# Nine phases of a transformer chain in one block: at each phase border a wait on one semaphore in place of a barrier of all engines

## The reference

```python
x = L0(x, ctx)          # one softmax over projected context rows, a gate, then a normalization
x = L1(x, ctx, mask)    # causal self-attention, cross-attention, gated feed-forward;
                        #   each token uses the "v" or the "l" weights, by the mask
x = L2(x, ctx, mask2)   # cross-attention with 16 heads of 64, then a feed-forward with gelu
x = L3(x, ctx, mask)    # as L1, with weights of its own
```

## Time and profile before

| what | value |
|---|---|
| median of 3 runs (lowest to highest) | 2504.32 us (2503.06 to 2508.76) |
| the profiled execution, its own time | 2509.57 us |
| its span, first to last instruction | 2507.8 us |
| granted TensorE clock, mean over the span (1 is 2.4 GHz, 0.5 is 1.2 GHz) | 0.96 |
| busy: PE, DVE, ACT, POOL | 2311.2, 1410.7, 1143.7, 653.1 us |
| moved by DMA | 85.55 MB |

### The profile page before, as it was taken

How to read it: one execution, slowest core, us unless ns; L and a number is a source line. 1 busy time by engine, 2 the same in 40 slices (tenths; PEclk the granted TensorE clock), 3 DMA queues, 4 the chain that set the end, 5 groups by cost and what they waited for, 6 DMA issues and landing times. The chain is left out here.

```text
span 2507.8 us, 63604 instructions
## 1 busy us (share of the span) xinstructions
PE 2311.2 (92%) x24286; PEld 1890.0 (75%) x24287; DVE 1410.7 (56%) x2866; ACT 1143.7 (46%) x2585; POOL 653.1 (26%) x833
## 2 busy tenths in 40 slices
PE   5994999997996999799999997998999998997998
PEld 4673788875765999688888876996888875666998
DVE  3563666664775333466666655554666665764433
ACT  2553444443664333334344344445444435664332
POOL 1333222212662222111111110001222214652222
PEclk9996999997998999899999998998999998998999
DMA  5440000002003111300000001000000002001111
GB/s 179 58 58 9 18 15 15 15 15 71 27 27 93 55 58 57 110 2 2 2 2 2 2 2 35 0 0 14 15 15 15 15 13 79 27 30 51 59 59 42
DMA packets 78468, 85.55 MB, mean 34 GB/s; under 512 B 19891, under 2 KB 69376, under 8 KB 78112
## 3 DMA queue, kind: packets, MB, share of 16 engines
q1 hardware_dynamic: 56016, 41.55, 7.3%
q10 hardware_dynamic: 13856, 19.61, 2.4%
q0 software_dynamic: 8368, 21.15, 2.4%
HBM read 52.22 MB, written 21.40 MB: 29 GB/s over the span
## 5 line engine op out<-in xcount | busy, mean ns | idle before, releaser
L1184 POOL TENSOR_TENSOR s_kx<-s_qkt,const 128x512 f32<-128x512 f32 x128 | 131.7, 1049 | 447.3 <-ACT s_qkt L1115 447.3
L2150 PE MATMUL ps_all<-f_wh,f_xh 128*128 x396 | 155.2, 392 | 10.6 <-DVE f_xl L2295 10.6
L1536 POOL TENSOR_TENSOR c_kx<-c_qkt,const 128x512 f32<-128x512 f32 x128 | 130.5, 1037 | 118.2 <-ACT c_qkt L1480 118.0
L534 POOL TENSOR_TENSOR a_probs<-a_probs,a_sm 128x1024 f32<-128x1024 f32 x32 | 60.9, 1902 | 384.6 <-DVE a_sm L529 384.6
L1123 ACT ACTIVATE s_pt<-ps_all 128x512 f32<-128x512 f32 x128 | 69.7, 594 | 186.9 <-PE ps_all L1005 186.9
L2151 PE MATMUL ps_all<-f_wh,f_xl 128*128 x396 | 149.3, 377 | 0.0
L2152 PE MATMUL ps_all<-f_wl,f_xh 128*128 x396 | 149.2, 377 | 0.0
L1874 ACT ACTIVATE self_w<-ps_all,a_q_bias 128x256 f32<-128x256 f32 x128 | 53.7, 470 | 196.5 <-PE ps_all L1722 196.5
L2290 DVE SCALAR_TENSOR_TENSOR f_h<-ps_all,rstd,f_act_g 128x688 f32<-128x688 f32 x66 | 61.6, 934 | 143.9 <-PE ps_all L2152 131.9
L2175 PE MATMUL ps_all<-f_dh,f_hh 128*128 x396 | 116.9, 295 | 4.0 <-DVE f_hl L2305 4.0
L505 DVE TENSOR_REDUCE s_mx<-ps_all 128x8 f32<-128x512 f32 x128 | 82.5, 686 | 61.3 <-PE ps_all L991 61.3
(11 more groups left out here) (322 smaller groups left out, 7518.7 us busy)
## 6 DMA issues: line engine op xcount, KB each, us to landing
s_v_swap<-s_v_own SPq DMA_DIRECT2D x128, 68.0 KB, 2.0
f_x_in<-x_sorted SPq DMA_DIRECT2D x66, 128.0 KB, 2.0
x_res<-x_sorted SPq DMA_DIRECT2D x66, 128.0 KB, 2.1
x_sorted<-x_res POOLq DMA_DIRECT2D x1, 4224.0 KB, 16.5
l_rows<-in_x SPq DMA_DIRECT2D x32, 128.0 KB, 3.6
x_res<-in_x SPq DMA_DIRECT2D x32, 128.0 KB, 7.4
x_res<-x_back SPq DMA_DIRECT2D x1, 3584.0 KB, 20.5
l_rows<-in_ctx SPq DMA_DIRECT2D x32, 64.0 KB, 4.3
```

The source lines that it names most:

```text
L1184: ins = nc.gpsimd.tensor_tensor(kx[:, p % 2, c], qkt[:, p % 2, 2 + c].rearrange("p (b k) -> p b k", b=2).unsqueeze(2) .broadcast_to([P, 2, ...
L1536: ins = nc.gpsimd.tensor_tensor(kx[:, p % 2, b], qkt[:, p % 2, 1, b * S:b * S + S].unsqueeze(1).broadcast_to([P, RH, S]), const[:, C_H8X:C ...
L2150: nc.tensor.matmul(bank, x_high, wh[:, w_at], start=(c == 0), stop=False)
```

## The change

All nine phases now stand in one block. Each engine's function of each phase begins with `previous_done(eng)`: a wait until `res_ok` has reached the value that the phases so far add up to, which is the last residual of the phase before (layer 0 has none before it and does not wait). The barriers at the eight inner borders are gone; the one behind the preparation and the one at the end stay. The rest of each phase is the same text, four columns further left. Cut to the pattern, with one phase of six functions:

```diff
@@ -256,6 +256,11 @@
+        def previous_done(eng):
+
+            if res_ok.base > 0:
+                eng.wait_ge(res_ok.handle, res_ok.at(0))
+
...
@@ in layer0, and alike in the five other phase functions @@
-                with nc.Block() as block:
-                    @block.sync
-                    def _(sp):
-                        def step(p, u):
+                @block.sync
+                def _(sp):
+                    previous_done(sp)
+                    def step(p, u):
...
-                    @block.gpsimd
-                    def _(pool):
+                @block.gpsimd
+                def _(pool):
+                    previous_done(pool)
...
-        for k, (phase, _) in enumerate(phases):
-            def load_next(eng):
-                if k + 1 < len(phases):
-                    phases[k + 1][1](eng, weights_in[(k + 1) % 2].handle)
-            phase(weights_in[k % 2], load_next)
+        with nc.Block() as block:
+            for k, (phase, _) in enumerate(phases):
+                def load_next(eng):
+                    if k + 1 < len(phases):
+                        phases[k + 1][1](eng, weights_in[(k + 1) % 2].handle)
+                phase(weights_in[k % 2], load_next)
```

More of the change, by code:

```diff
@@ new lines, in _, with spread, rstd_, put_sorted @@
+                @block.gpsimd
+                def _(pool):
+                    previous_done(pool)
+                    nc.gpsimd.memset(eps_f[:], CHD * 1e-6).then_inc(hpad_ok.handle, 1)
+                    def spread(p):
+                        pool.wait_ge(qkt_ok.handle, qkt_ok.at(p + 1))
+                        if s_pe.due(p - 1):
+                            pool.wait_ge(s_pe.handle, s_pe.at(p - 1))
+                        for b in range(2):
+                            ins = nc.gpsimd.tensor_tensor(
+                                kx[:, p % 2, b],
+                                qkt[:, p % 2, 1, b * S:b * S + S].unsqueeze(1).broadcast_to([P, RH, S]),
+                                const[:, C_H8X:C_H8X + RH].unsqueeze(2).broadcast_to([P, RH, S]), ALU.mult)
+                        ins.then_inc(kx_ok.handle, 1)
+                    def rstd_(g):
+                        pool.wait_ge(stat_ok.handle, stat_ok.at(g * G + G))
+                        if g == 0:
+                            pool.wait_ge(hpad_ok.handle, hpad_ok.at(1))
+                        cols = slice(g * G, g * G + G)
+                        nc.gpsimd.tensor_tensor(power[:, cols], power[:, cols], eps_f[:], ALU.add) \
+                            .then_inc(eps_ok.handle, 1)
+                        pool.wait_ge(eps_ok.handle, eps_ok.at(g + 1))
+                        nc.gpsimd.tensor_tensor(factor[:, cols], power[:, cols], half_neg[:], ALU.pow) \
+                            .then_inc(rstd_ok.handle, 1)
+                    def put_sorted(p):
+                        pool.wait_ge(res_ok.handle, res_ok.at(p + 1))
+                        pool.indirect_dma_start(x_sorted, bass.IndirectOffsetOnAxis(slot_i[:, p:p + 1], 0),
+                                                x_tile(p), None).then_inc(sorted_put.handle, 16)
+                    spread(0)
+                    spread(1)
+                    rstd_(0)
+                    for p in range(PAIRS + 3):
+                        if has(p + 2):
+                            spread(p + 2)
+                        if has(p) and p % G == G - 1 and has(p + 1):
+                            rstd_(p // G + 1)
+                        if has(p - 3):
+                            put_sorted(p - 3)
@@ new lines, in _ @@
+                @block.sync
+                def _(sp):
+                    previous_done(sp)
+                    sp.wait_ge(back_put.handle, back_put.at(0))
+                    back = x_back.rearrange("(n p) d -> p n d", p=P)
+                    for k, (lo, hi) in enumerate(((0, 4), (4, PAIRS))):
+                        sp.dma_start(x_res[:, lo * D:hi * D].rearrange("p (n d) -> p n d", d=D), back[:, lo:hi]) \
+                            .then_inc(back_in[k].handle, 16)
+                @block.tensor
@@ L1793, in dense @@
-                        def dense(p):
-                            pe.wait_ge(o_ok.handle, o_ok.at(p + 1))
-                            for c in range(J):
-                                high, low = oh[:, c * D:c * D + D], ol[:, c * D:c * D + D]
-                                nc.tensor.matmul(ps_d[:, 0:D], oth[:, c], high, start=(c == 0), stop=False)
-                                nc.tensor.matmul(ps_d[:, 0:D], oth[:, c], low, start=False, stop=False)
-                                ins = nc.tensor.matmul(ps_d[:, 0:D], otl[:, c], high, start=False, stop=(c == J - 1))
-                            ins.then_inc(d_pe.handle, 1)
@@ new lines, in _ @@
+                            proj_q(g + 1, 2 * i + 1)
+                            proj_k(g + 1, 2 * i)
+                        if has(p - 1):
+                            pv(p - 1)
+                        if more:
+                            proj_k(g + 1, 2 * i + 1)
+                        if has(p + 1):
+                            proj_v(p + 1)
+                        if i == 1 and has_group2(g + 2):
+                            xt_(g + 2)
+                        if has(p - 1):
+                            if p == 1:
+                                pe.wait_ge(wlow_ok.handle,
+                                           wlow_ok.at(len(q_splits) + len(k_splits) + len(o_splits)))
+                            dense(p - 1)
@@ new lines, in _, with rstd_ @@
+                @block.gpsimd
+                def _(pool):
+                    previous_done(pool)
+                    def rstd_(g):
+                        pool.wait_ge(stat_ok.handle, stat_ok.at(2 * g + 2))
+                        nc.gpsimd.tensor_tensor(var[:], mv[:, :, 1], eps5[:, 0:2], ALU.add).then_inc(eps_ok.handle, 1)
+                        pool.wait_ge(eps_ok.handle, eps_ok.at(g + 1))
+                        if xn_ok.due(2 * g):
+                            pool.wait_ge(xn_ok.handle, xn_ok.at(2 * g))
+                        nc.gpsimd.tensor_tensor(inv_std[:], var[:], half_neg[:, 0:2], ALU.pow).then_inc(rstd_ok.handle, 1)
+                    rstd_(0)
+                    rstd_(1)
+                    for p in range(PAIRS):
+                        softmax_norm(pool, sm, probs, p, p % 2)
+                        if p % 2 == 0 and has_group2(p // 2 + 2):
+                            rstd_(p // 2 + 2)
@@ new lines, in _ @@
+                @block.sync
+                def _(sp):
+                    previous_done(sp)
+                    sp.wait_ge(sorted_put.handle, sorted_put.at(PAIRS))
+                    for t in range(NT):
+                        if t >= 2:
+                            sp.wait_ge(xt_pe.handle, xt_pe.at(t - 1))
+                            sp.wait_ge(tile_in[t % 2].handle, tile_in[t % 2].at(t // 2))
+                        sp.dma_start(x_in[:, t % 2], x_sorted[t * P:t * P + P, :]).then_inc(tile_in[t % 2].handle, 16)
+                        sp.dma_start(rows(t), x_sorted[t * P:t * P + P, :]).then_inc(tile_in[t % 2].handle, 16)
+                    if store:
+                        sp.wait_ge(back_put.handle, back_put.at(NT))
@@ new lines, in _, with rstd_, put_back @@
+                @block.gpsimd
+                def _(pool):
+                    previous_done(pool)
+                    for e in range(2):
+                        at = (e * IC + full) * D
+                        nc.gpsimd.memset(dh[:, at:at + D].bitcast(F32), 0.0)
+                        nc.gpsimd.memset(dl[:, at:at + D].bitcast(F32), 0.0)
+                    for u in range(2):
+                        ins = nc.gpsimd.memset(h[:, u, I:IC * P], 0.0)
+                    ins.then_inc(hpad_ok.handle, 1)
+                    def rstd_(t, u):
+                        pool.wait_ge(stat_ok.handle, stat_ok.at(t + 1))
+                        nc.gpsimd.tensor_tensor(stat[:, u, 1:2], stat[:, u, 0:1], eps6[:, 0:1], ALU.add) \
+                            .then_inc(eps_ok.handle, 1)
+                        pool.wait_ge(eps_ok.handle, eps_ok.at(t + 1))
+                        if h_ok.due(t - 1):
+                            pool.wait_ge(h_ok.handle, h_ok.at(t - 1))
+                        nc.gpsimd.tensor_tensor(rstd[:, u, 0:1], stat[:, u, 1:2], half_neg[:, 0:1], ALU.pow) \
+                            .then_inc(rstd_ok.handle, 1)
+                    def put_back(t):
+                        pool.wait_ge(res_ok.handle, res_ok.at(t + 1))
+                        if n == 1 and t == 0:
+                            pool.wait_ge(home_in.handle, home_in.at(1))
+                        to = out_flat if store else x_back
+                        pool.indirect_dma_start(to, bass.IndirectOffsetOnAxis(home_i[:, t:t + 1], 0), rows(t), None,
+                                                bounds_check=TOK - 1, oob_is_err=False).then_inc(back_put.handle, 16)
+                    rstd_(0, 0)
+                    rstd_(1, 1)
```

(5 more changed lines are left out.)

2897 lines of the change are left out of this document (1402 added, 1495 removed).

## The result

The changed kernel takes 2486.49 us (median of 4 runs, 2485.96 to 2486.99), the kernel before in the same comparison 2505.38 (2503.06 to 2508.76): a ratio of 0.9924, 95% interval 0.9906 to 0.9941, or 18.9 us less. Forecast were 2480 and 24.4 us. The profiled executions differ by more: 2509.57 against 2486.78, spans 2507.8 against 2485.0, so 22.8 us. The sum was made against these, and so the reading by borders is too.

The account below looks back on a forecast made before the run. TensorE, busy 92% of the span, bounds the phases, so only borders can gain: 11.0 + 8.4 + 4.0 + 1.0 = 24.4 us off 2504.3, about 2480; own range 2477 to 2484, widened to 2475 to 2491 for 8 in 10.

Parts of the forecast that it names:

- Border 1, 11.0 us: POOL's memset follows its last DMA issue, so the `s_power` sum starts at 220.5, not 231.55; bounds 3.2 and 13.8.
- The copy's row: Earlier in border 1's phase, copy L850 starts at 197.40, right at a DMA issue's end: POOL goes on before landing.
- The port that POOL and DVE share: Border 1: DVE's split L1267 meeting POOL's DMA issue or memset, costed at nothing; at most 1.02 us if fully blocked.
- Borders 3 and 8, 4.2 us each: ACT's weight split starts 4.2 us earlier and sets the start; 8.4 for both, bounds 1.5 and 4.3 each.
- the landing rival: At borders 3, 4 and 8 the DMA landing binds, each gains only about 1.5 us: 2487.8 us; 6%.
- Border 4, 4.0 us: ACT's weight loads start 4.7 us earlier, SP's `x_back` reads 1.6 earlier, first statistics sooner; bounds 0 and 4.7.
- the bound of 0: Border 4's low end: the put sits behind all the weight loads, which costs what the earlier start brings.
- the bytes' reckoning: Border 4: 3.1 us head start at 399 GB/s clears 1.24 MB of loads, so the read lands up to 3.1 sooner.
- Borders 2, 5, 6 and 7, 1.0 us: Barrier of 0.29 us less the wake-up, some 0.25 each, 1.0 together; bounds 0 and 1.2.
- two rivals that did not come: POOL still holds at border 1 (2487.7 us, 8%); the DMA landing binds at 3, 4 and 8 (2487.8, 6%).
- The slower rival: Behind border 1 TensorE's clock stays low through self-attention's first four pairs: 44.4 us more, 2524.3 us; 3%.

Follow-up runs that it names:

- the last version: Changed kernel with POOL's `home_d` DMAs early and ACT's first weight loads at borders 1, 2, 4 to 7 issued by SP: 2459.19 us, 0.9813 of before.

## Why the prediction was right, and where it was wrong

**Border 1, 11.0 us: right**, in the order of the engines too (POOL last, at 220.61 for 220.5). From the residual's end the `s_power` sum moved from 17.96 to 6.72 us, a gain of 11.24, of which 10.64 arrive at the first residual. The 0.6 between fits the clock, though no run shows it apart: the granted clock came back to 1.00 only 9.7 us behind TensorE's first product there (before: some 7.5), with 6.43 us of products at the lower level in place of 4.18. Table of stretches from the first product (before: 0.1 us behind it) to the clock's return and on, of the changed kernel, then of before (columns as in the earlier trace rows):

```profile
223.30:233.00 9.70, 6.43 (x17) 4.86 (x18) 4.75 (x6) 6.60 (x16) 1.42 (x3) 0.50 0.00 0
233.00:243.00 10.00, 9.46 (x71) 7.54 (x69) 5.30 (x10) 4.75 (x10) 2.61 (x3) 0.99 0.09 23
```

```profile
234.50:242.00 7.50, 4.18 (x12) 3.14 (x13) 4.74 (x6) 6.57 (x16) 0.69 (x2) 0.50 0.00 0
242.00:250.00 8.00, 7.69 (x46) 6.46 (x45) 3.35 (x7) 2.64 (x6) 2.78 (x4) 0.98 0.08 19
```

The reason given, that POOL joined the barrier only when its DMAs had landed, was most of it but not all. What held POOL was its drain at the block's end, which the orders of instructions shown for before do not list: they have only the branch and the barrier's wait. It ended 1.4 us behind the last landing (218.60 + 7.2), and in the run with early `home_d` DMAs it took some 3 us, and held POOL for 2.43 of the 13.8, though the last of 32 DMAs had been issued 60 us before (in the kernel before they land within 9 us). The copy's row was the right evidence: within a block POOL goes on behind a DMA. The port that POOL and DVE share cost nothing: the split beside a DMA issue kept its 1.02 us, and L1211, now clear of it, took 0.20 as in the earlier trace rows. Where the two meet again, in the last version at 215.78, POOL's takes 0.57 and ends 0.06 us behind DVE's, as at border 1 of before; that agrees with the rule of the Trainium skill (SBUF — State Buffer, "SBUF: two separate sides"), by which one of the two has the pair for its whole instruction.

**Borders 3 and 8, 4.2 us each: right in mechanism.** ACT's split moved by 4.26 and 4.30 us and sets the start; the landing rival fell. Border 3 has 3.81 at the first residual; where the other 0.4 went was not followed up. Border 8 has 6.67: the stretch of 30 us behind the residual had a mean granted clock of 0.66 before, 0.80 in the changed kernel and 0.77 in the run with early `home_d` DMAs, in this order (columns as in the earlier trace rows):

```profile
2258.20:2288.20 30.00, 15.93 (x67) 13.26 (x68) 14.24 (x18) 15.39 (x27) 5.89 (x15) 0.66 0.16 50
```

```profile
2242.10:2272.10 30.00, 20.01 (x110) 17.30 (x111) 16.89 (x22) 17.84 (x32) 9.12 (x18) 0.80 0.20 62
```

```profile
2242.50:2272.50 30.00, 15.62 (x79) 13.10 (x80) 15.28 (x21) 16.21 (x28) 7.96 (x16) 0.77 0.17 53
```

In that run the border keeps its barrier and still saves 2.28 us; from it to the changed kernel it saves another 4.39. So about 2.3 of the 6.67 are TensorE's clock coming back sooner, and 4.4 the barrier.

**Border 4, 4.0 us: the step that failed.** The prediction added two terms: SP's read of `x_back` starts 1.6 us sooner, and with the loads' head start it lands up to 3.1 sooner behind its issue. The second came: from SP's issue to the first statistics it is 4.08 us in place of 7.65. The first came out the other way round: the put's landing went from 2.3 to 6.8 us, and SP's read starts 2.87 later behind the residual. Together that is the 0.70, near the bound of 0 that the prediction had named itself for a put that sits behind the loads. It took the value near the bytes' reckoning, which counted bytes over the same engines and left out their order: the read cannot begin before the put lands, so what delays the put delays all behind it. The run with the loads behind the reads gives 4.12 back; the run without this barrier alone shows no gain.

**Borders 2, 5, 6 and 7, 1.0 us: too much.** The first instructions start 0.04 us behind the residual's end where it was 0.29, but the next residual keeps 0.11, 0.00, -0.12 and -0.09. At border 2 ACT issues its loads from 575.94 to 583.17, 7.23 us, where it took 7.08 before; TensorE waits for ACT behind that. For the other three the record shows no such row.

**The sum.** In the profiles 22.8 stands against 24.4, which is nearer than the terms were, and that is luck: border 4 lacks 3.75, the four small ones 1.1, borders 1 and 3 together 0.75, while the clock gave 2.1 inside self-attention 1 and some 2.3 at border 8, which no term had. Without these two gifts it would be 18.4. For self-attention 1 the last 30 us show it, of before (in its second profile, with 1.25 in place of 2.14, the clock is 0.83), then of the changed kernel:

```profile
557.90:587.90 30.00, 22.77 (x292) 16.22 (x290) 12.31 (x26) 7.84 (x16) 2.06 (x2) 0.76 0.03 6
```

```profile
545.40:575.40 30.00, 22.78 (x362) 16.99 (x356) 14.33 (x31) 7.84 (x16) 2.06 (x2) 0.87 0.03 6
```

In the medians the saving is 18.9, because both profiles of before are among its longer executions; the forecast took a saving read from one execution off a median. So 2486.49 us lies outside the 2477 to 2484 that the forecast gave as its own range, and inside the 2491 to which it was widened for two rivals that did not come. The longer executions of before tend to the lower granted clock; what brings it about stays open, as no profile fell among the shorter ones.

**The slower rival** did not come: the clock was back within 20 us of the residual at border 1. Its mechanism is there in small: 2.25 us more of busy TensorE at half speed, some 1.1 us in place of 44.4.

## What to carry to other kernels

Before a barrier is priced, see who comes last to it: here it cost 0.1 to 0.3 us of its own, and 4 to 14 where an engine drained its DMA queue in front of it. Issuing that engine's DMAs early took as much off border 1 as taking out the barrier did. Once a border has no barrier, the next engine's first rows are the bound: with the barriers gone, moving weight loads from ACT to SP and POOL's DMAs ahead brought 27.3 us more, some 4 of them by the clock at borders 2 and 7, where taking out the barriers had brought 18.9. A transfer that is let go sooner must be checked against the transfers that others wait for: put it behind them.

## What was not expected of the hardware

In most of these runs POOL's drain behind indirect DMAs took time for each one issued since the drain before, also where they had long been issued: some 0.08 us each, read from 32 (2.63 us more than with none at border 2), 33 (2.75 from the last issue's end, at border 4 of before), 65 (5.30 more at border 5) and 97 (8.0). This does not go on without end: the last drain of the changed kernel, with 162 indirect DMAs since the one before, takes 3.97 us, and that of the run with a barrier at border 1, with 130, 3.96, as in the kernel before with 33. Why is open.

The granted clock's low stretches behind a border are not fixed. Behind border 8, with the same instructions and the barrier in place, TensorE's clock came back so much sooner in the run with early `home_d` DMAs than in both profiles of before that 2.3 us hung on it. The only edit lies some 2000 us ahead; how it, or chance, brings this about is open.
